# Delta rule: dot products summed by selection matmuls instead of folds and reductions

## The reference

```python
hk = jnp.concatenate([relu(hk), relu(-hk)], axis=-1)        # 64 -> 128 features
hq = jnp.concatenate([relu(hq), relu(-hq)], axis=-1)
hk, hq = _mul_roll_repeat(hk), _mul_roll_repeat(hq)         # x*roll(x,1), x*roll(x,2)
hk = hk / hk.sum(-1, keepdims=True); hq = hq / hq.sum(-1, keepdims=True)
denom_acc = jnp.cumsum(hk, axis=2)
key_denom = einsum('bhsd,bhsd->bhs', key_denom_shifted, hk) # 1 at step 0
hb = hb * key_denom; hk = hk / (key_denom + EPS)
denominator = einsum('bhsd,bhsd->bhs', denom_acc, hq)
def step(W, inp):
    q_t, k_t, v_t, b_t = inp
    new_v = b_t * (v_t - einsum('bhd,bhdv->bhv', k_t, W))
    W = W + einsum('bhd,bhv->bhdv', k_t, new_v)
    return (W, einsum('bhd,bhdv->bhv', q_t, W))
```

## Time and profile before

| | us |
|---|---|
| median of 3 runs | 3754.56 (3752.11 to 3755.17) |
| profiled execution, span of its instructions | 3773.4 |
| wload, in that execution | 2527 to 2557 |
| dots | 2557 to 3244 |
| alg | 3244 to 3307 |

### The profile page before, as it was taken

One profiled execution on the slowest core, in us unless ns is written; L12 is line 12 of the kernel. 1 busy time (PEld: TensorE's weight loads), 2 busy tenths in 40 slices (PEclk: granted clock), 3 DMA queues, 4 the chain that ended last, 5 costly groups with the idle time before them and its releaser, 6 DMA issues. The chain is left out here.

```text
span 3773.4 us, 30406 instructions
## 1 busy us (share of the span) xinstructions
PE 2844.9 (75%) x9408; PEld 1533.5 (41%) x9416; DVE 2125.6 (56%) x3711; ACT 1247.3 (33%) x1958; POOL 1004.1 (27%) x636
## 2 busy tenths in 40 slices
PE   2016898999999799999678776827899889477317
PEld 1003444555555444444344432514444444256303
DVE  7997432222222465664544483126777777477687
ACT  1003433111111266666443211414444444133103
POOL 0003654000000000000233203035889989200004
PEclk7558999999999899999788888967999999689658
DMA  1002121000000275544000110120000000000000
GB/s 50 0 0 46 46 62 45 0 0 0 0 0 0 57 154 143 144 139 138 5 0 1 29 41 31 49 67 14 0 1 0 1 0 0 22 1 1 2 0 29
DMA packets 106418, 124.34 MB, mean 33 GB/s; under 512 B 21771, under 2 KB 59788, under 8 KB 106028
## 3 DMA queue, kind: packets, MB, share of 16 engines
q1 hardware_dynamic: 104236, 118.56, 12.1%
q0 software_dynamic: 2048, 4.20, 0.4%
HBM read 108.55 MB, written 14.16 MB: 33 GB/s over the span
## 5 line engine op out<-in xcount | busy, mean ns | idle before, releaser
L2306 POOL TENSOR_TENSOR dots_pr<-dots_g 128x1536 f32<-128x1536 f32 (+1 forms) x129 | 394.3, 3096 | 100.2 <-DVE dots_g L2411 60.2
L2332 PE MATMUL dots_fold<-dots_pr,all_ident 128*128 128x512 f32 x688 | 323.7, 617 | 2.7 <-ACT dots_pr L2372 2.7
L1012 DVE SCALAR_TENSOR_TENSOR attn_sim<-attn_sc,attn_mask 128x512 f32<-128x512 f32 (+3 forms) x256 | 125.9, 492 | 316.9 <-PE attn_sc L938 313.8
L938 PE MATMUL attn_sc<-attn_q,attn_xb 128*128 128x512 f32 (+3 forms) x768 | 295.0, 486 | 0.0
L949 PE MATMUL attn_op<-attn_sim,attn_v 128*128 128x512 f32 (+3 forms) x768 | 295.0, 486 | 0.0
L1298 DVE TENSOR_TENSOR grp_h<-grp_sq,grp_cb 128x512 f32<-128x512 f32 x256 | 176.5, 692 | 192.0 <-ACT grp_sq L1186 171.7
L1126 PE MATMUL grp_po<-grp_h,grp_down 128*128 128x512 f32 x512 | 266.5, 602 | 6.0 <-DVE grp_h L1298 5.9
L1118 PE MATMUL grp_ph<-all_xt,grp_up 128*128 128x512 f32 x512 | 263.9, 598 | 0.5 <-ACT grp_sg L1202 0.5
L2408 DVE TENSOR_TENSOR dots_m<-dots_pu,dots_sg 128x512 f32<-128x512 f32 x256 | 164.7, 685 | 143.5 <-ACT dots_sg L2363 136.5
L1180 ACT ACTIVATE grp_r<-grp_ph 128x512 f32<-128x512 f32 x272 | 162.4, 597 | 185.5 <-PE grp_ph L1118 183.8
L2372 ACT ACTIVATE dots_pr<-dots_pr 128x1536 f32<-128x1536 f32 (+1 forms) x129 | 169.3, 1337 | 159.3 <-POOL dots_pr L2306 159.3
(11 more groups left out here) (605 smaller groups left out, 5035.1 us busy)
## 6 DMA issues: line engine op xcount, KB each, us to landing
grp_cb<-grp_combine SPq DMA_DIRECT2D x512, 128.0 KB, 3.2
mix_cb<-top_weights SPq DMA_DIRECT2D x64, 256.0 KB, 3.2
cap_xs<-cap_zero SPq DMA_DIRECT2D x7, 320.0 KB, 4.9
experts_xe<-cap_xs SPq DMA_DIRECT2D x7, 320.0 KB, 3.4
all_x<-in_L_attn_x_dram SPq DMA_DIRECT2D x4, 512.0 KB, 5.4
cap_w<-in_L_ffn_W_dram SPq DMA_DIRECT2D x1, 2048.0 KB
cap_ys<-experts_yo SPq DMA_DIRECT2D x8, 256.0 KB, 2.3
delta_h<-all_xn SPq DMA_DIRECT2D x1, 2048.0 KB
```

The source lines that it names most:

```text
L938: nc.tensor.matmul(sc[k % SC][:, 0:w], xb[:, m * P:(m + 1) * P], q[:, par, n0:n0 + w], start=True, stop=True).then_inc(s_mm, 1)
L2306: nc.gpsimd.tensor_tensor(slot[U % SLOTS][:, r0 + i0:r0 + i0 + n], g[:, I % 2, a0:a0 + n, hs], key, ALU.mult).then_inc(pp_ready, 1)
L2332: ins = nc.tensor.matmul(fold[U % NU][:].rearrange("p (n h f) -> p n h f", h=HQ, f=FW), ident[:], slot[U % SLOTS][:, :, :, f * FW:(f + 1) ...
```

## The change

The layout of the stage dots turns round. Features stand on the partitions: two heads of 64 (a chunk; there are 8), and 512 positions in the free dimension (the even or the odd blocks, `par`). A pass I is one chunk and one parity, so there are again 16. `wE` holds three versions of each chunk's weights, shifted by 0, 1 and 2. A feature is three matmuls of 512 columns into three of five PSUM banks (`bank`), a sign of the first, and the same four VectorE operations. The matmul that refills a bank waits for its last reader: the third one of feature n needs feature n-1 finished.

A pass has 12 units of 4 rows of 512: four only take absolute values (ScalarE, for the norms), six are products on GpSimd, two are products on VectorE (positions 3 and 8). ScalarE clips the eight products. There are five buffers (three `dots_pr`, two halves of `XN`). For each unit TensorE makes four matmuls with `sel`, a 0/1 matrix of 32 columns that adds up the partitions of a head and places the sum in the row of that head; the four quarters of positions go to PSUM partitions 0, 32, 64 and 96 of one bank of `sums`. The sums collect over 8 passes; ScalarE copies them out after pass 7 and after pass 15, and SyncE moves them by 16 DMAs each time into `dots`, which now has block and head on the partitions. The norms and collects on VectorE go.

In alg, beta comes from 8 matmuls into 32-row tiles, VectorE waits for it only after the reciprocal and the first scaling, and the clearing of `alpha` goes. `alpha` is solved as `alphaT`; ten transposes on TensorE and three copies on ScalarE bring it back.

```diff
     with Stage(nc, "delta") as s:
-        wE = s.sb("wE", [P, 2, NH, XP])
+        wE = s.sb("wE", [P, 2, NCH, SHIFTS, P])
...
-        dots = s.sb("dots", [P, ROWS, JT, NH])
...
+        sel = s.sb("sel", [P, NCH, 2, Q32])
+        dots = s.sb("dots", [P, ROWS, P])
...
+                        nc.gpsimd.affine_select(out=half, in_=half, compare_op=ALU.not_equal, fill=1.0, base=-h2,
+                                                pattern=[[-2, NCH], [-NH, 2], [1, Q32]], channel_multiplier=0).then_inc(sel_made, 1)
...
+                            src = pw[part * 2 + half][:].rearrange("p (a h d) -> p a h d", h=2, d=D_)
+                            for sh in range(SHIFTS):
+                                dst = wE[:, part, half * 4:(half + 1) * 4, sh].rearrange("p a (h d) -> p a h d", h=2)
+                                if sh:
+                                    nc.scalar.activation(dst[..., D_ - sh:], src[..., 0:sh], ACT.Copy, scale=-1.0)
+                                last = nc.scalar.activation(dst[..., 0:D_ - sh], src[..., sh:], ACT.Copy)
...
+                    for par in range(2):
+                        nc.scalar.activation(wb2[:, par, par * NH:(par + 1) * NH], pw[6][:, 0:NH], ACT.Copy).then_inc(w_copied, 1)
...
+            XB = 5
+            SLOTS = 5
...
+            PIECES = (((0, 1, 4),), ((0, 5, 3), (3, 7, 1)), ((1, 3, 4),), ((1, 7, 1), (2, 5, 3)))
+            UNITS = [("abs", 0, 0), ("abs", 1, 0), ("pool", 0, 0), ("dve", 2, 0), ("pool", 1, 0), ("pool", 3, 0),
+                     ("abs", 0, 1), ("pool", 0, 1), ("dve", 2, 1), ("abs", 1, 1), ("pool", 1, 1), ("pool", 3, 1)]
...
+            g = s1.sb("g", [P, 2, 2, NF, GROUP])
...
+            pr = s1.sb("pr", [P, OWN, 4, GROUP])
...
+            spare = XN[:].rearrange("p (k n q) c -> p k n (q c)", k=2, n=4)
+            slot = [pr[:, k] for k in range(OWN)] + [spare[:, k] for k in range(SLOTS - OWN)]
...
+            def factors(I, pos, piece):
+                _, u, sh = UNITS[pos]
+                s_, a0, n = PIECES[u][piece]
...
+                        for pos in made_by["pool"]:
...
+                            for piece in range(len(PIECES[UNITS[pos][1]])):
...
+                                nc.gpsimd.tensor_tensor(slot[w % SLOTS][:, at:at + n], a_, b_, ALU.mult).then_inc(pool_ready, 1)
...
+                        par, a = divmod(I, NCH)
+                        for sh in range(SHIFTS):
...
+                                if kind == 0:
+                                    pe.wait_ge(g_ready, before + 1)
+                                else:
+                                    pe.wait_ge(m_ready, 2 * before + kind)
+                            nc.tensor.matmul(bank(n, sh)[:], wE[:, 1 - k % 2, a, sh], XTj[:, k // 2, par::2], start=True, stop=True).then_inc(u_mm, 1)
...
+                    def unit(I, pos):
...
+                        par, a = divmod(I, NCH)
...
+                        g_, b_ = (u, 2) if kind == "abs" else divmod(u, 2)
+                        pe.wait_ge(unit_ready, w + 1)
...
+                        for jj in range(JJ):
+                            ins = nc.tensor.matmul(sums[b_][jj * Q32:(jj + 1) * Q32, :], sel[:, a, g_], slot[w % SLOTS][:, :, jj * P:(jj + 1) * P],
+                                                   start=(a == 0 and pos == mates[0]), stop=(a == NCH - 1 and pos == mates[-1]))
+                        ins.then_inc(unit_mm, 1)
...
                         feature(0, k)
...
                     for I in range(NI):
...
-                            folds(I, 0, 2 * k, 2 * k + 2)
...
-                        folds(I, 1, 0, 2)
...
-                        folds(I, 1, 2, FOLD)
-                        feature(I + 2, 0)
-                        feature(I + 2, 1)
-                        folds(I, 2, 0, FOLD)
-                        folds(I, 3, 0, FOLD)
+                        for q in range(4):
+                            feature(I + 1, 2 * q)
+                            feature(I + 1, 2 * q + 1)
+                            for pos in range(3 * q, 3 * q + 3):
+                                unit(I, pos)
...
+                        act.wait_ge(u_mm, SHIFTS * n + 1)
...
-                    def clip(I, u):
...
+                            act.wait_ge(m_ready, 2 * (n - 1))
+                        nc.scalar.activation(sg[:, n % 2], bank(n, 0)[:], ACT.Sign).then_inc(sg_ready, 1)
...
+                    def unit(I, pos):
...
+                        v_ = slot[w % SLOTS]
+                        if kind == "abs":
+                            act.wait_ge(g_ready, NF * (I + 1))
...
+                            nc.scalar.activation(v_, g[:, I % 2, sh, u::2], ACT.Abs).then_inc(unit_ready, 1)
...
+                        if kind == "pool":
+                            act.wait_ge(pool_ready, I * NPOOL + pool_upto[pos])
+                        else:
+                            act.wait_ge(dve_ready, I * NDVE + made_by["dve"].index(pos) + 1)
...
+                        nc.scalar.activation(v_, v_, ACT.Relu).then_inc(unit_ready, 1)
...
+                    def sums_out(par):
+                        act.wait_ge(unit_mm, (par + 1) * NCH * NU)
...
+                        for k in range(3):
+                            nc.scalar.activation(ev[:, k], sums[k][:], ACT.Copy).then_inc(ev_ready, 1)
...
+                        if I == NCH:
+                            sums_out(0)
+                        unit(I, 0)
+                        sign(I + 1, 0)
+                        unit(I, 1)
+                        sign(I + 1, 1)
+                        for pos in (2, 3, 4):
+                            unit(I, pos)
                         sign(I + 1, 2)
                         sign(I + 1, 3)
-                        clip(I, 2)
...
-                        clip(I, 3)
-                        sign(I + 2, 0)
-                        sign(I + 2, 1)
...
-                            clip(I + 1, 0)
-                            clip(I + 1, 1)
+                        for pos in (5, 6, 7):
+                            unit(I, pos)
+                        sign(I + 1, 4)
+                        sign(I + 1, 5)
+                        for pos in (8, 9, 10):
+                            unit(I, pos)
+                        sign(I + 1, 6)
+                        unit(I, 11)
+                        sign(I + 1, 7)
+                    sums_out(1)
...
+                    for par in range(2):
+                        sp.wait_ge(ev_ready, 3 * (par + 1))
+                        for jj in range(JJ):
+                            for g_ in range(2):
+                                src = ev[jj * Q32 + g_ * NH:jj * Q32 + (g_ + 1) * NH]
+                                dst = dots[(2 * jj + par) * NH:(2 * jj + par + 1) * NH]
+                                sp.dma_start(dst[:, 8 * g_:8 * (g_ + 1)].rearrange("p r n -> p (r n)"), src[:, 0:2].rearrange("p b n -> p (b n)")).then_inc(moved, 16)
+                                sp.dma_start(dst[:, NORM + S * g_:NORM + S * (g_ + 1)].rearrange("p r n -> p (r n)"), src[:, 2]).then_inc(moved, 16)
+                    sp.wait_ge(moved, 2 * 16 * 4 * JJ)
...
+                        if k == 0 and I >= 2:
+                            dve.wait_ge(pool_ready, NPOOL * (I - 1))
+                            dve.wait_ge(unit_ready, NU * (I - 1))
...
+                        if n >= 2:
+                            dve.wait_ge(g_ready, n - 1)
+                        for sh in range(1, SHIFTS):
+                            dve.wait_ge(u_mm, SHIFTS * n + sh + 1)
+                            tt(m[:, n % 2, sh - 1], bank(n, sh)[:], sg[:, n % 2], ALU.mult).then_inc(m_ready, 1)
+                        for sh in range(1, SHIFTS):
+                            dve.wait_ge(m_ready, 2 * n + sh)
+                            ins = stt(g[:, I % 2, sh - 1, k], m[:, n % 2, sh - 1], 0.0, bank(n, 0)[:], ALU.max, ALU.mult)
...
+                    def products(I, pos):
...
-                        redu(dots[:, NORM:NORM + NF, j, hh * HH:(hh + 1) * HH], g[:, I % 2], AX.X, ALU.add, apply_absolute_value=True).then_inc(n_ready, 1)
...
-                    def collect(I, u):
...
-                        redu(dots[:, second * 8:(second + 1) * 8, j, h0:h0 + HQ], fold[u][:].rearrange("p (n h f) -> p n h f", h=HQ, f=FW),
-                             AX.X, ALU.add).then_inc(d_ready, 1)
...
+                        tt(slot[w % SLOTS], a_, b_, ALU.mult).then_inc(dve_ready, 1)
...
                     for I in range(NI):
                         feature(I + 1, 0)
...
-                        collect(I - 1, 3)
...
+                        products(I, made_by["dve"][0])
+                        for k in range(1, 5):
                             feature(I + 1, k)
-                        collect(I, 0)
...
-                        norms(I + 1)
-                        collect(I, 1)
-                        collect(I, 2)
-                    collect(NI - 1, 3)
...
-        alpha = s.sb("alpha", [P, S, S, JT, NH])
```

(17 more changed lines are left out.)

215 lines of the change are left out of this document (89 added, 126 removed).

## The result

| | before | after |
|---|---|---|
| median (range) | 3754.86 (3752.11 to 3756.86) | 3725.03 (3718.90 to 3733.71) |
| ratio, 95% interval | | 0.9921 (0.9903 to 0.9940) |
| profiled execution, span | 3773.4 | 3719.6 |

A forecast was written before the change was run, and what follows sets the result against it. It took TensorE and GpSimd, both nearly full and waiting for each other, as the bound, and after the change a loop closed once a pass. Terms -13 + 4 + 7 + 1 - 2 - 13 = -16 gave 3739 us, range 3703 to 3805.

The forecast's parts named there:

- Tiles (12 x 0.86): TensorE in a dots pass: four 32-column tiles run at once, 0.86 us a unit, 10.3 for 12 units.
- Turns: VectorE's two products a pass and GpSimd's operations take turns at SBUF, costing GpSimd 4.4 us a pass.
- The walk: Step-by-step timing of one dots pass through all engines' written order, ending with feature 7 at 40.1 us, rounded to 40.0.
- Rival (a): In dots, VectorE's products hide without taking turns: pass 38.0 us, 30 us more saved, 3709; chance 8%.
- The loop (-13): Dots passes: a loop across engines, closed once a pass, gives 40.0 instead of 40.9 us, 15 times.
- Rival (b): In dots, the second product meets a longer GpSimd operation or the walk is too tight: +15 to +51 us; chance 25%.
- Fill (+7): Start of dots, before the first pass: three matmuls a feature at a low clock make it 7 us longer (0 to +20).
- Weights (+4): ScalarE's copies of the weights in wload: 1.54 us for 0.54, four times, 4 us longer.
- pass 8 (+1): Three ScalarE copies of the sums, 1.8 us, mostly in front of an existing wait, make pass 8 1 us longer.
- End of the stage (-2): Last pass to the end of dots, with 16 DMAs issued 0.46 apart: 47.5 us instead of 49.7.
- Solver (-13): Stage alg: beta's matmuls hide under reciprocal and scaling and the clearing goes, -13.7; an exposed copy leaves -13 us.

The follow-up runs named there:

- e2: Changed kernel with each unit's four matmuls put into two 64-column tiles instead of four of 32: 3834.13 us, ratio 1.0155 to the kernel before.
- e1: Changed kernel with GpSimd computing the short piece of units 4 and 10 before the long one: 3763.18 us, ratio 0.9965 to the kernel before.
- e6: Changed kernel with VectorE's two products a pass replaced by a one-operand multiplication by 1.0: 3692.53 us, one execution.
- e10: The kernel of e1 run again beside e9 on one chip: 3737.66 us, ratio 0.9956 to the kernel before.
- e9: The changed kernel run again, unaltered, beside e10 on one chip: 3727.64 us, ratio 0.9935 to the kernel before.
- e8: Changed kernel reordered, GpSimd's wait relaxed, pass 15's eight products on VectorE, last 16 DMAs from two queues: 3620.80 us, ratio 0.9654 to the kernel before.
- e7: Changed kernel with VectorE waiting for beta ahead of the reciprocal in alg: 3726.57 us, one execution; alg 54.4 instead of 50.3.
- e3: Changed kernel with only the order of signs, features and units altered on ScalarE, TensorE and VectorE: 3671.57 us, ratio 0.9727 to the kernel before.

## Why the prediction was right, and where its sizes were off

**Tiles (12 x 0.86), right.** 0.87 a unit, and e2 shows what two at a time would have been.

**Turns, right.** The walk had the first product asked at 5.4 and run from 8.1 to 10.3; it was asked at 5.3 and ended at 10.1, and the second did not wait. e1 shows that this wait is not on the loop's path, as in the walk, where GpSimd's pieces give the same 2.2 either way. The second product is another matter. The walk let GpSimd's unit 11 wait for it, to 28.2. Unit 11 starts at 27.74, just behind the product, but its 2.19 us of idle time is put down to TensorE's sums, and in e6, where the second operation is over 1.1 us before unit 11 starts, the idle time is 2.19 as well. What holds unit 11 is its buffer, and only the first product costs GpSimd time (3.33 instead of 1.26). Rival (a) is open only as a price: no run had the products and no turns.

**The loop (-13), right in its mechanism, 9 too small.** The walk's order holds step by step (t after 2679.91, walk against trace): feature 4 25.8 / 25.5, second product 28.2 / 27.7, sign 6 34.5 / 33.7, feature 7 40.1 / 39.4. The step that was mis-sized is the adding up of recorded durations, 1.91 for each ScalarE operation. Operations in a row on one engine overlap at their ends in the record: 2707.64 to 2713.06 holds three of them and is 5.42, 1.81 each. GpSimd's likewise start 4.51 and 3.42 apart (2679.91, 2684.42, 2687.84) where the walk took 4.6 and 3.5, so unit 7 ends at 20.4 and not at 20.7. Together this is 0.7 a pass at feature 7. The walk itself ended at 40.1 and was entered as 40.0, so 0.6 of it stands in the 15 passes, 9 us.

**Rival (b), not met.** The second product was asked for as unit 10 ended, as in the walk, and its record of 2.33 shows hardly a wait. The late starts that it needed did not occur. (The middle of its +15 to +51 gives 3772, not the 3765 written there; the forecast does not use it.)

**Fill (+7), 4 too large.** The step that failed is the clock: the prediction priced the first two features at 1.2 GHz, since PEclk was 0.66 there before; it is 1.00 in the window above. 2.1 to VectorE's first operation, 2.6 for the first feature and seven of 3.1 come to 26.4 of the 26.6. (In e1, e2, e6 and e10 the same fill took 28.3; in e10 its PEclk was 0.94.)

**Weights (+4), right**; **pass 8 (+1)**, 0.7, but not for the reason given. Windows of pass 8 in the kernel after, then in e9, the same kernel:

```profile
2876.98:2917.12 40.14, 35.21 (x148) 11.39 (x144) 24.91 (x34) 27.77 (x24) 29.79 (x11) 0.96 0.12 20
```

```profile
2876.83:2916.20 39.37, 33.51 (x148) 11.06 (x144) 24.74 (x34) 27.77 (x24) 29.80 (x11) 1.00 0.12 21
```

Both have the copies of the sums, and where the clock stays at 1.00 the pass is 39.4 like the others. The copies cost nothing there; the 0.7 came with the lost clock.

**End of the stage (-2), 1.5 too large.** 16 DMAs were issued 0.63 apart, not 0.46, 10 us instead of 7.4; the rest of the term was 1.1 too large. Its 1.5 for waits on slots came from no row. e8 shows what sharing the issues out brings.

**Solver (-13), right**, 13.4; the cover held and e7 prices it.

**The sum.** -16 against -28 by the stages: 9 of the 12 is the loop with pass 8 and 4 the fill, less 1.5 for the end. The direction and the mechanism were right; the size, 30 where 16 was forecast, was not. The range (3703 to 3805) held the time. What the prediction named as its signs stands in the traces: GpSimd's 6.96 us for the last feature, ScalarE's wait for GpSimd at unit 7, the reciprocal at the start of alg (3202.74).

**What the prediction did not see** is that the loop was a choice. It walked the written order, found 40 us on engines busy for 25 to 32, and took that as the kernel's nature. e3 took 5.2 us a pass out of it by the order alone.

## What to carry to other kernels

When every engine is lighter than the pass is long, look for the loop that is closed once a pass, walk it, and then move each small operation that starts a long chain (a sign, a narrow matmul) ahead of the long ones in its queue: here that brought more than twice what the change itself did. When adding operations up along such a loop, take the distance from start to start of neighbours in the trace, not the recorded duration. A stage's last pass has other free engines than the loop has, so its work may be shared out differently.

## What the runs showed of the hardware

- Four float32 matmuls of 512 columns into four 32-column tiles take 0.87 us, as long as one of full width; into two 64-column tiles 1.74. The trace of the kernel before shows only two at a time.
- Each change between a 128-column and a 32-column tile on TensorE costs about 0.17 us (3.77 for 3.44 of work with two changes).
- In the middle passes TensorE kept 2.4 GHz with gaps of 1.35 and 1.51 us, and fell to 1.2 GHz for a part of nine of the 13 passes with one gap of about 2.5 in their place (e10; a window behind one such gap has PEclk 0.50). The cost was 1.0 us in each of the nine. The four others kept 2.4 GHz. The changed kernel lost it behind other gaps: in pass 0 (PEclk 0.96) behind 2.10 and 1.96, where the pass was 39.4 all the same, and in pass 8 behind 2.16, where e9 kept it behind 2.15.
- A VectorE operation with one SBUF operand (multiplication by a constant, 2048 elements in 1.26 us) takes turns with GpSimd just as one with two operands does: it is recorded at 3.75 behind a GpSimd operation in flight, and GpSimd's next 512 elements take 2.27 instead of 1.26 (e6).
